# Reordering the queues of a fused attention and mixture-of-experts layer

## The reference

```python
h = _layernorm(x, axis=-1) * (1 + ca) + sa
x = x + ga * _L0_attn_ref(h, ...)     # gate ga held away from zero
h = _layernorm(x, axis=-1) * (1 + cb) + sb
x = x + gb * _L0_ffn_ref(h, ...)
```

```python
xk = x_prev + (x - x_prev) * tmk          # likewise xv, xr
p = jnp.maximum(pp, ww)
e1 = jnp.exp(pp - p); e2 = jnp.exp(ww - p)
out = (e1 * aa + e2 * vt) / (e1 * bb + e2)
# the state aa, bb, pp goes on with the decay
...
rwkv = jax.nn.sigmoid(r) * wkv
out = jnp.einsum('bth,oh->bto', rwkv, Wo) + bo
```

## Time and profile before

| | |
|---|---|
| Median of 3 runs | 409.97 us (407.69 to 410.45) |
| Profiled execution | 408.2 us, its span 406.3 us |
| Busy: TensorE, weight load | 366.6 us (90%), 224.8 us |
| Busy: VectorE, ScalarE, GpSimd | 334.6 us (82%), 295.2 us (73%), 44.7 us |
| Mean granted TensorE clock | 0.958 |
| Chain that ended last | TensorE 63%, ScalarE 22%, VectorE 9%, issue 3% |

### The profile page before, as it was taken

One profiled execution on the slowest core, in us unless ns is written; L12 is line 12 of the kernel. 1 busy time (PEld: TensorE's weight loads), 2 busy tenths in 40 slices (PEclk: granted clock), 3 DMA queues, 4 the chain that ended last, 5 costly groups with the idle time before them and its releaser, 6 DMA issues.

```text
span 406.3 us, 4276 instructions
## 1 busy us (share of the span) xinstructions
PE 366.6 (90%) x1348; PEld 224.8 (55%) x1348; DVE 334.6 (82%) x667; ACT 295.2 (73%) x466; POOL 44.7 (11%) x76
## 2 busy tenths in 40 slices
PE   4892873999999999999999999999999999969985
PEld 4561332756565845675476646574567455725752
DVE  4799989987989898999899898989898988541541
ACT  2699699846997589948994799759985894324332
POOL 4030013001400050002200230005000200010000
PEclk9995795799999999999999999999999999969999
DMA  8900010001000110011000300011001000100011
GB/s 287 268 5 1 0 52 0 0 2 52 0 2 0 52 52 2 0 52 54 0 2 2 103 0 0 2 53 50 2 1 52 2 0 0 52 2 0 0 53 52
DMA packets 15626, 13.27 MB, mean 33 GB/s; under 512 B 4690, under 2 KB 15092, under 8 KB 15604
## 3 DMA queue, kind: packets, MB, share of 16 engines
q1 hardware_dynamic: 15572, 12.99, 10.4%
q10 hardware_dynamic: 32, 0.01, 0.0%
HBM read 8.80 MB, written 4.19 MB: 32 GB/s over the span
## 4 chain that ended last, share of the span: by engine, by line
PE 63%; ACT 22%; DVE 9%; issue 3%; DMA 1%; SPq 0%; DVEq 0%; ACTq 0%
PE mm L737 29%; PE mm L632 10%; PE yo L765 7%; PE yo L650 7%; ACT arg L391 6%; ACT n_xn L326 5%; PE yo L659 3%; ACT arg L417 3%; ACT pool_x L366 2%; ACT h_h L365 2%; ACT kv L374 2%; DVE h_l L979 2%; ACT arg L405 1%; PE cb L749 1%; DVE mixed L879 1%
## 5 line engine op out<-in xcount | busy, mean ns | idle before, releaser
L632 PE MATMUL mm<-mixed,WT 128*128 128x512 f32 x192 | 87.5, 604 | 8.1 <-DVE mixed L879 8.1
L765 PE MATMUL yo<-act,w_dn 128*128 128x512 f32 x160 | 74.1, 613 | 5.4 <-DVE act L1056 5.4
L632 PEld LDWEIGHTS mm<-mixed,WT 128*128 128x128 f32 x192 | 36.3, 193 | 53.4 <-issue 39.6
L737 PE MATMUL mm<-h_h,w_up_h 128*128 128x512 f32 x160 | 55.2, 426 | 4.3 <-DVE h_l L979 4.3
L765 PEld LDWEIGHTS yo<-act,w_dn 128*128 128x128 f32 x160 | 30.8, 197 | 41.9 <-issue 35.6
L737 PE MATMUL mm<-h_l,w_up_h 128*128 128x512 f32 x160 | 51.1, 401 | 0.0
L737 PE MATMUL mm<-h_h,w_up_l 128*128 128x512 f32 x160 | 51.0, 400 | 0.0
L300 POOL TENSOR_TENSOR n_ve<-n_mv,small 128x4 f32<-128x4 f32 x16 | 8.2, 510 | 310.9 <-DVE n_mv L868 310.9
L374 ACT ACTIVATE kv<-mm,cols 128x512 f32<-128x512 f32 x32 | 21.8, 682 | 18.9 <-PE mm L632 18.9
L737 PEld LDWEIGHTS mm<-h_h,w_up_h 128*128 128x128 f32 x160 | 28.4, 192 | 12.6 <-DVE h_l L979 6.4
L737 PEld LDWEIGHTS mm<-h_h,w_up_l 128*128 128x128 f32 x160 | 30.6, 191 | 7.5
(11 more groups left out here) (149 smaller groups left out, 662.6 us busy)
## 6 DMA issues: line engine op xcount, KB each, us to landing
x_in<-in_L_attn_x_dram SPq DMA_DIRECT2D x8, 512.0 KB, 3.5
out_dram<-pool_x SPq DMA_DIRECT2D x5, 512.0 KB, 2.9
pool_x<-in_L_wmod_dram SPq DMA_DIRECT2D x2, 512.0 KB, 4.9
out_dram<-x_third SPq DMA_DIRECT2D x2, 512.0 KB, 2.9
pool_x<-in_L_wmod_dram SPq DMA_DIRECT2D x2, 256.0 KB, 4.0
pool_g<-in_L_ffn_Wg_dram SPq DMA_DIRECT2D x2, 256.0 KB, 5.0
pool_g<-in_L_ffn_Wu_dram SPq DMA_DIRECT2D x2, 256.0 KB, 4.4
w_dn<-in_L_ffn_Wd_dram SPq DMA_DIRECT2D x1, 512.0 KB, 3.9
```

The costliest lines, as they stand in the source:

```text
L632: last = nc.tensor.matmul(mm[PROJECT_BANK[j]][:, :], WT[:, w, kc, oc * P:(oc + 1) * P], mixed[:, w, kc, :], start=(kc == 0), stop=(kc == K ...
L737: last = nc.tensor.matmul(mm[UP_BANK[i]][:, :], w[:, kc, gu, e * P:(e + 1) * P], rhs[:, kc, :], start=(n == 0), stop=(n == 3 * KH - 1))
L765: last = nc.tensor.matmul(yo[oc][:, :], w_dn[:, e, oc * P:(oc + 1) * P], act[:, e, :], start=(e == 0), stop=(e == NB - 1))
```

## The change

Six edits:

1. From step 2 on, the orders on TensorE, ScalarE and VectorE are new (`step`); steps 0 and 1 have functions of their own (`first_step`, `second_step`) that keep most of the old order. To allow it, `attn`, `turn_attn`, `turn_down`, `turn2` and `tanh_r` take a half as an argument, and their waits are cut accordingly. The routing is split at more places.
2. VectorE ends a step with `out_sums` 0, 3, 2; `low_part`, `out_sums` 1 and 4 open the next one.
3. ScalarE applies `affine2(prev)` ahead of `normalise1(nxt)`.
4. `x_in` has three buffers instead of two, so a chunk's load waits for the residual of three chunks earlier.
5. Chunk 0's norm is done as (x - mean) * rstd, without the two GpSimd operations that make the shift; its turn stands ahead of that of weight K.
6. WT of Wo is copied by ScalarE (activation with scale -0.5) instead of VectorE; the other weights by `tensor_copy`.

The core of the diff:

```diff
@@ TensorE: the new step
+            def step(n):
+                before, prev, cur, nxt = (chunk(n + d) for d in (-2, -1, 0, 1))
+                turn1(nxt, 0)
+                up(prev, 0)
+                logits(prev)
+                turn1(nxt, 1)
+                up(prev, 1)
+                up(prev, 2)
+                turn_logits(prev)
+                up(prev, 3)
+                up(prev, 4)
+                attn(cur, 0)
+                project(nxt, (0,))
+                attn(cur, 1)
+                project(nxt, (1,))
+                turn_down(before, 0)
+                up(prev, 5)
+                turn_down(before, 1)
+                turn_comb(prev)
+                turn_attn(cur, 0)
+                up(prev, 6)
+                spread_comb(prev, 1)
+                up(prev, 7)
+                spread_comb(prev, 2)
+                up(prev, 8)
+                up(prev, 9)
+                spread_comb(prev, 3)
+                spread_comb(prev, 4)
+                turn_attn(cur, 1)
+                project(nxt, (2, 3, 4))
+                down(prev, 0)
+                turn2(cur, 0)
+                turn2(cur, 1)
+                project(nxt, (5,))
+                down(prev, 1)
@@ ScalarE: start of the new step
+                affine2(prev, 0)
+                affine2(prev, 1)
+                normalise1(nxt)
+                reciprocal_seed(cur)
+                affine1(nxt, 0)
+                nc.scalar.preload_act_table_set(SILU_SET)
+                tanh_r(cur, 0)
+                affine1(nxt, 1)
+                logits_out(prev)
+                tanh_r(cur, 1)
+                silu(prev, 0)
...
@@ VectorE: the new step
+                low_part(prev)
+                out_sums(cur, 1)
+                out_sums(cur, 4)
+                divide(cur, 0)
...
+                scan_max(nxt, 1)
+                weigh(prev, 2)
+                gate_up(prev, 3)
+                residual1(cur, 0)
+                gate_up(prev, 4)
+                weigh(prev, 3)
+                residual1(cur, 1)
+                weigh(prev, 4)
+                stats2(cur)
+                scan_sums(nxt, 0)
+                stats1(after)
+                scan_sums(nxt, 1)
+                out_sums(nxt, 0)
                 out_sums(nxt, 3)
-                out_sums(nxt, 4)
+                out_sums(nxt, 2)
@@ loads
-                wait(sp, x1_done, 2 * (c.n - 1))
-                sp.dma_start(x_in[c.half][:, :, :], x_chunks[c.n]).then_inc(x_loaded[c.half], 16)
+                wait(sp, x1_done, 2 * (c.n - 2))
+                sp.dma_start(x_in[c.n % 3][:, :, :], x_chunks[c.n]).then_inc(x_loaded[c.n % 3], 16)
```

More of the change, by code:

```diff
@@ L296, in rstd @@
             def rstd(norm, c):
+                direct = norm is norm1 and c.n == 0
+                step = 3 * c.n - (2 if norm is norm1 and c.n else 0)
                 wait(pool, norm.mv_done, TT * (c.n + 1))
@@ L331, in normalise1 @@
             def normalise1(c):
-                normalise(norm1, x_in[c.half], c)
+                normalise(norm1, x_in[c.n % 3], c)
             @of_chunk
@@ L503, in first_step, with second_step @@
                 output_exponential(nxt, 3)
-            def step(n):
-                before, prev, cur, nxt = (chunk(n + d) for d in (-2, -1, 0, 1))
-                normalise1(nxt)
+            def second_step():
+                prev, cur, nxt = (chunk(n) for n in range(3))
                 affine2(prev, 0)
                 affine2(prev, 1)
+                normalise1(nxt)
                 reciprocal_seed(cur)
@@ L786, in step @@
                 up(prev, 4)
[L787 to L793 removed]
+                attn(cur, 0)
+                attn(cur, 1)
+                project(nxt, (0, 1))
                 up(prev, 5)
@@ L841, in _ @@
             turn(norm1, chunk(0), 1, cb)
+            turn_square(K, mm[2])
             turn_square(V, mm[3])
@@ L1093, in first_step, with second_step @@
                 out_sums(nxt, 4)
-            def step(n):
-                before, prev, cur, nxt, after = (chunk(n + d) for d in (-2, -1, 0, 1, 2))
-                divide(cur, 0)
-                divide(cur, 1)
-                divide(cur, 2)
-                divide(cur, 3)
+            def second_step():
+                prev, cur, nxt, after = (chunk(n) for n in range(4))
+                for n in range(4):
+                    divide(cur, n)
                 mix(nxt, 0)
@@ L1125, in step @@
                 out_sums(nxt, 0)
-                out_sums(nxt, 1)
-                low_part(cur)
+                out_sums(nxt, 3)
                 out_sums(nxt, 2)
+            def step(n):
+                before, prev, cur, nxt, after = (chunk(n + d) for d in (-2, -1, 0, 1, 2))
+                low_part(prev)
+                out_sums(cur, 1)
+                out_sums(cur, 4)
+                divide(cur, 0)
+                divide(cur, 1)
+                divide(cur, 2)
+                divide(cur, 3)
+                gate_up(prev, 0)
+                route(prev, 0, 4)
+                mix(nxt, 0)
+                route(prev, 4, 9)
+                gate_up(prev, 1)
+                route(prev, 9, 12)
+                mix(nxt, 1)
+                route(prev, 12, ROUTE_STEPS + 1)
+                scan_max(nxt, 0)
+                residual2(before, 0)
+                mix(nxt, 2)
+                residual2(before, 1)
+                gate_up(prev, 2)
+                weigh(prev, 1)
+                scan_max(nxt, 1)
[7 more added lines that the diff above has]
+                stats2(cur)
+                scan_sums(nxt, 0)
+                stats1(after)
+                scan_sums(nxt, 1)
+                out_sums(nxt, 0)
                 out_sums(nxt, 3)
-                out_sums(nxt, 4)
+                out_sums(nxt, 2)
             for e in range(E):
```

197 lines of the change are left out of this document (118 added, 79 removed).

## The result

| | before | after |
|---|---|---|
| median of the runs | 410.15 us (407.69 to 410.45, 4 runs) | 424.40 us (423.87 to 424.81, 4 runs) |
| profiled execution, span | 408.2 us, 406.3 us | 424.45 us, 422.6 us |
| mean granted clock | 0.958 | 0.951 |

A forecast was written before the change was run, and what follows sets the result against it. A middle step was taken as bound by TensorE, busy for all but 0.62 of 43.70 us. Gains of 1.1 through step 6 and 4.9 in the last two made 6.0 us: 404.0 us on the median's scale, range 399.5 to 409.3.

The forecast's parts named there:

- Head: Start of the kernel: first part mix 0.3 us earlier, Wo's copy off VectorE 0.5; together 0.8 us gained.
- First handover: Into step 1: a third input buffer ends VectorE's 1.69 us wait for chunk 2's data; 2.5 us ahead with the head.
- Inside step 1: TensorE waits about 0.3 us at `turn_logits` for the late logits' copy on ScalarE, leaving 2.2 us ahead.
- Second handover: Into step 2: den behind `low_part` stalls TensorE 1.5 us at `turn1(nxt, 1)`; 1.4 given back, 0.8 ahead.
- Handovers into steps 3 to 6: Middle steps: a stall of 0.4 to 0.6 us replaces the old 0.6; 0.3 us gained for all.
- GpSimd's price: Norm ahead of `turn2`: 3.5 us for GpSimd's four operations, pow 1.86 beside a scan; hidden with 0.5 us to spare.
- Last two steps: Steps 7 and 8: shorter waits and full clock for step 7's down products, less a new stall; 4.9 us gained together.
- (d): Slower: new 1.5 us stalls at each handover bring the granted clock down each time; 425 us, chance 0.07.
- (a): Handover loop looser than walked: den ready 0.6 us sooner in steps 3 to 6; 400.6 us, chance 0.17.
- (b): Handover loop tighter: each of four handovers costs the 1.5 us of the second; 407.6 us, chance 0.13.
- (c): Clock falls in one of step 7's gaps of 1.7 and 1.4 us; 405.5 to 406.9 us, chance 0.09.
- (e): Reordered tail does nothing, another wait (attention out, routing) holding the weights; 408.9 us, chance 0.08.

The follow-up runs named there:

- Den early: Changed kernel, but VectorE ends second and later steps with `out_sums` 0 and 1 and opens the next with `low_part`, 2, 3, 4: 397.75 us.
- the two-buffer run: Changed kernel with steps ending in `out_sums` 0 and 1, and `x_in` in two buffers instead of three: 398.88 us, ratio 0.9737 to the kernel before.
- the statistics first: Changed kernel with VectorE doing `stats1(after)` directly behind `stats2(cur)`, ahead of both `scan_sums`: 405.31 us, ratio 0.9876 to the kernel before.

## Why the prediction was wrong, point by point

- **What bounds.** Right for what it was read from, and it misled: a middle step had little idle, so little could be won, but nothing in that view says how much can be lost. It was also not quite true that only 0.62 us could be won. Den early's step is 1.0 us shorter, 0.6 from the stall; the rest was inside TensorE's busy time, and no run shows what it was.
- **Head, 0.8 us.** About 0.6 came. The first mix is at 14.35 (14.17 foretold, 14.49 before), but its start varies from 13.79 to 15.58 between executions of the same head. From there to the first `divide` it is 23.3 us in the five runs with the new head whose first 24 projection instructions took 10.57 us, and 23.8 in the two with the old head: 0.5, as foretold. In the execution shown these took 12.29 us, which makes the `divide` 1.3 later (38.95, before 38.30). 12.0 to 12.4 and 10.57 both occur with either head, so that is a difference between executions.
- **First handover, 1.7 more.** Nearly right in size, its cause wrong. From the first `divide` to the first gate/up product it is 31.00 us (30.7 to 32.1 in the runs with this order), before 32.41: 1.4 us. The wait for x_in near 59 us is gone, as foretold, but by the swap of `stats1` and `scan_sums` 0, which the prediction does not mention there; the two-buffer run shows it.
- **Inside step 1, 0.3 given back.** It was 1.0: from the first gate/up product of step 1 to that of step 2 46.01 us pass (69.95 to 115.96), before 45.05. TensorE waits 0.18 us at `turn_logits`, where 0.3 stood in the sum, and 0.63 us at the third gate/up product for `tanh_r`, which stood nowhere.
- **Second handover, stall of 1.5 us.** Right: 1.39 us for hT at 119.95, and the clock stayed at 1.00.
- **Handovers into steps 3 to 6, gain 0.3.** This is the step that failed. It walked VectorE and ScalarE operation by operation, and its sum has no term for `normalise1`, as if that were always ready when ScalarE came to it. The chain of `stats1` over GpSimd to `normalise1` was put at nothing without a walk, though the swap had moved it 3 us towards its user and under other work on VectorE. There GpSimd's last operation took 6.78 us, `normalise1` waited 4.61 and TensorE 3.71. Where the walk was right it can be seen once GpSimd is let in: with the statistics first TensorE waits for hT at these handovers, 0.5 and 0.7 us, where 0.4 to 0.6 stood in the prediction, and the time is 405.3 against 404.0. So the missing term is 424.4 less 405.3 = 19.1 us, all but 1.3 of the miss. In the traces the rest shows as small shortfalls: with the statistics first, steps 2 to 6 take 1.9 us more than before, where 1.1 stood in the sum, beside the 0.7 of step 1 and the 0.4 of the tail. But "gain nothing there" was too dark for another order: den early removes these stalls.
- **GpSimd's price.** The earlier trace rows gave 1.86 us beside a scan for pow, and that price held (1.86 again). I took the dearest row as the bound for anything that GpSimd does. The new neighbours were not scans but a row of plain 128x1024 operations without a gap, which no row of before shows beside GpSimd; there the price is no multiple of a duration but the time to the next opening. The Trainium skill, page "SBUF — State Buffer", section "Who interferes with whom", was cited at `turn2`, with the verdict that by its rule the sum was the same. It names exactly the pair that met: a VectorE instruction with two SBUF inputs, a GpSimd one that reads SBUF. But where it says how long the other is blocked (of VectorE's two-port modes), that is for the whole of one instruction. By that the price would have been about 1.1 us (an estimate, from the distance of two such operations); the runs with an opening behind the first show 1.10, and the changed kernel 6.78.
- **Last two steps, 4.9 us.** Right but for step 8: 4.4 came. Idle 1.75 us (1.7 foretold) before down products at full clock, the new stall of the turn 1.20 (1.4), step 7 to step 8 35.05 us, before 39.5 (4.6 foretold for step 7); from there to the end 34.3 us, before 34.2, where 0.3 was foretold. Undoing VectorE's part of step 7 costs 3.9 us in the traces; of the 4.6, the 0.96 for attention is not touched by it, so 3.6 is the number to set beside it.
- **Rivals.** (d) stood for slower, at 425 us, and 424.4 was measured, with a falling clock at each handover. That is luck: its stalls were to be 1.5 us long and to bring the clock down by themselves. The 1.39 us stall at step 2 left it at 1.00; it fell behind 3.71 us of idle that (d) did not know of. (a), (b), (c) and (e) did not happen: with GpSimd let in, the race was as walked. A rival for the chain through GpSimd was missing, and so the range was too narrow.

## What to carry to other kernels

When an order changes, walk every chain that ends at the waiting engine, those through the idle engine too: an engine that was busy 11% of the time was what came to set the loop. Ask of each small GpSimd operation on a critical chain what VectorE does beside it; a dependency between neighbours, or a memset of one column, in a row of two-input operations can be worth far more than its own time (here 19.1 us for 0.06). And a step that gains little on paper is no safe step: price what it makes late as well as what it makes early.

## What was not expected of the hardware

- A GpSimd operation of 0.20 us took 6.78 us beside six VectorE operations of 128x1024 back to back, 3.37 us when a memset of 0.06 us stood behind the third, and 1.10 us when it stood behind the first or when the second operation read the result of the first. Beside scans of 128x512 in a row it got in within 1.10 us, and the same kind of operation took 0.20 us beside statistics in a row. Why an opening as short as this is enough, and whether a row of large operations with one SBUF input, or with one in PSUM, would hold GpSimd as well, was not tried.
- The granted clock, at 1.00 before, fell behind 3.71 us (and 3.80, 4.48) of TensorE idle, and stayed at 1.00 behind 1.20 to 1.75 us.
- The first 24 projection instructions took 10.57 us in some executions and 12.0 to 12.4 in others of kernels with the same head; that costs 1.3 us of the 5.2 between the fastest and the slowest of 13 runs of the kernel before (408.43 to 413.67). In the changed kernel's trace the weight loads of the first few take 0.34 us and come every 0.86 us, where later ones take 0.19 and come every 0.43, as at half clock, though the granted clock is recorded as 1.00. What decides it is open.
